# A graph network on one core: another place in ScalarE's queue for the copy of vector parts, and another wait for every second group of gathers

## What is computed

```
# first layer, per edge
x = silu(edge_radial @ W1 + b1)           # "layer 1": 8 -> 64
x = silu(x @ W2 + b2)                     # "layer 2": 64 -> 64
tpw = x @ W3 + b3                         # "layer 3": 64 -> 256 = W00, W110, W01, W10, each 8 x 8
hs_e, hv_e = h[src, :8], h[src, 8:]       # the gather: scalars, vectors of the source node
m0 = ALPHA * (einsum(hs_e * sh0, W00) + INV_SQRT3 * einsum(hv_e, sh1, W110))
m1 = ALPHA * (einsum(hs_e, sh1, W01) + einsum(hv_e * sh0, W10))
agg = segment_sum(concat(m0, m1), dst) / 4
x = layernorm(x + (h_self + agg))
# second layer
e = leaky_relu((x @ a1)[src] + (x @ a2)[dst])
x = layernorm(x + segment_softmax_sum(e, x[src], dst))
```

## Time and profile before

| | |
|---|---|
| median of 3 runs | 8619.93 us (8616.9 to 8624.02) |
| the profiled execution's own time | 8616.82 us |
| its span, first to last instruction | 8615.0 us |
| PE busy over the span | 6996.6 us (81%) |
| DVE busy | 6416.2 us (74%) |
| POOL busy | 5314.4 us (62%) |
| ACT busy | 2833.3 us (33%) |
| mean granted TensorE clock | 0.839 of full speed |

### The profile page before, as it was taken

How to read it: one execution, slowest core, us unless ns; L and a number is a source line. 1 busy time by engine, 2 the same in 40 slices (tenths; PEclk the granted TensorE clock), 3 DMA queues, 4 the chain that set the end, 5 groups by cost and what they waited for, 6 DMA issues and landing times.

```text
span 8615.0 us, 93580 instructions
## 1 busy us (share of the span) xinstructions
PE 6996.6 (81%) x26126; PEld 5354.8 (62%) x26126; DVE 6416.2 (74%) x11130; ACT 2833.3 (33%) x4982; POOL 5314.4 (62%) x5400
## 2 busy tenths in 40 slices
PE   6788888888787778888887715999999999999992
PEld 4555555555555555555555414888888888888881
DVE  7777777777777777777777734777777777777774
ACT  4444544454545445444444300111111111111110
POOL 5555555555556655555555466666666666666666
PEclk7777777777777777777777757999999999999996
DMA  2211212121212112111111211222222222222221
GB/s 61 40 39 39 41 39 40 39 41 38 40 38 41 38 39 41 39 39 31 34 33 33 48 24 35 48 52 48 49 50 47 52 47 52 48 52 47 52 48 27
DMA packets 318657, 363.23 MB, mean 42 GB/s; under 512 B 157446, under 2 KB 259510, under 8 KB 317962
## 3 DMA queue, kind: packets, MB, share of 16 engines
q0 software_dynamic: 175840, 136.07, 12.1%
q1 hardware_dynamic: 142794, 226.94, 8.4%
HBM read 251.38 MB, written 111.20 MB: 42 GB/s over the span
## 4 chain that ended last, share of the span: by engine, by line
PE 48%; issue 22%; DVE 14%; POOL 5%; DMA 5%; ACT 3%; another core or an unknown queue 2%; DVEq 0%; ACTq 0%; POOLq 0%; SPq 0%
PE tpw L661 26%; PE tpw L593 9%; DMA early<-in_x_wide,idx 5%; POOL early L476 4%; PE hid L661 4%; PE hid L583 4%; PE hid L579 3%; PE hid L602 2%; DVE prod L962 2%; DVE prod L953 2%; DVE hot L1253 1%; ACT hid L678 1%; ACT early L684 1%; POOL msgs L476 1%
## 5 line engine op out<-in xcount | busy, mean ns | idle before, releaser
L476 POOL DMA_INDIRECT early<-in_x_wide,idx x2870 | 2777.0, 968 | 2002.1 <-issue 1999.7
L476 POOL DMA_INDIRECT prod<-table,idx x2125 | 2144.8, 1009 | 1064.0 <-issue 592.8
L661 PE MATMUL tpw<-highs,hot 128*128 128x462 f32 x6125 | 2310.9, 377 | 91.7 <-DVE prod L1268 43.1
L661 PE MATMUL tpw<-lows,hot 128*128 128x462 f32 x6125 | 2291.1, 374 | 23.2 <-issue 22.1
L593 PE MATMUL tpw<-w3s,early 128*128 128x256 f32 x6252 | 2084.3, 501 | 3.1 <-DVE prod L962 3.1
L593 PEld LDWEIGHTS tpw<-w3s,early 128*128 128x128 f32 x6252 | 1545.1, 255 | 714.6 <-issue 357.9
L661 PEld LDWEIGHTS tpw<-highs,hot 128*128 128x128 f32 x6125 | 1165.3, 190 | 265.4 <-issue 60.7
L661 PEld LDWEIGHTS tpw<-lows,hot 128*128 128x128 f32 x6125 | 1158.9, 189 | 173.6 <-issue 45.7
L583 PE MATMUL hid<-hid,w2s 128*128 128x384 f32 x1042 | 559.7, 624 | 621.9 <-ACT hid L678 607.5
L684 ACT ACTIVATE early<-hid,b2s 64x384 f32<-64x384 f32 x1042 | 601.8, 578 | 1319.9 <-PE hid L583 1153.0
L579 PE MATMUL hid<-early,w1s 16*128 16x384 f32 x1044 | 663.0, 725 | 372.6 <-issue 193.1
(11 more groups left out here) (186 smaller groups left out, 8011.5 us busy)
## 6 DMA issues: line engine op xcount, KB each, us to landing
big<-qrows SPq DMA_DIRECT2D x126, 512.0 KB
scan<-prod SPq DMA_DIRECT2D x125, 425.0 KB
scan<-sums SPq DMA_DIRECT2D x130, 384.0 KB, 2.6
early<-in_x_wide,idx POOLq DMA_INDIRECT x2870
prod<-table,idx POOLq DMA_INDIRECT x2125
qbx<-qx SPq DMA_DIRECT2D x131, 128.0 KB
early<-in_radial_t SPq DMA_DIRECT2D x262, 48.0 KB
sh<-in_sh SPq DMA_DIRECT2D x131, 48.0 KB
```

The costliest lines, as they stand in the source:

```text
L476: return pool.indirect_dma_start(out=dest, out_offset=None, in_=source, in_offset=bass.IndirectOffsetOnAxis(ap=index, axis=0))
L661: mm = pe.matmul(found[i % BANKS][:, 0:BC], hot(c)[:, g, at:at + P], split(s, g), start=g == 0 and s == 0, stop=g == NBATCH - 1 and s == S ...
```

## The change

It has two parts. On ScalarE, `spread_hv` of a half no longer stands ahead of `first_hidden` at the end of the half before; it stands one step later, directly behind the `hidden` that belongs to layer 2 of the half's own odd group. On POOL, the gathers of an odd group g no longer wait until layer 3 of group g - 2 is done (`tpw_ready`); they wait until layer 1 of group g - 1 is done (`layers_done`). The wait for `tpw_used` is kept for all groups, and the even groups keep both waits.

```
             def gather_again(it, k, m, loads, all_tiles=False):
                 pool.wait_ge(tpw_used, it * SLOTS + k - 1)
-                pool.wait_ge(tpw_ready, it * SLOTS + k - 1)
+                if k % HALF == 0:
+                    pool.wait_ge(tpw_ready, it * SLOTS + k - 1)
+                else:
+                    pool.wait_ge(layers_done, it * SLOTS + k)
...
             def iteration(it, m, before, searching, loads=None):
...
                     hidden(g + 1, (k + 1) % 2)
+                    if k % HALF == 0:
+                        spread_hv(it, h, it > 1 if isinstance(it, int) else True)
                     if k == 0 and before is not None:
                         collect(it - 2, m, before, CT)
...
                         one_hot_x(it, m, loads, ((0, 1), (2, 3), (4, 5), (6,))[k])
-                    if k % HALF == HALF - 1:
-                        spread_hv(it + 1 if h else it, 1 - h, h == 0 and before is not None or h == 1 and not first and not last,
-                                  last and h == 1)
                     first_hidden(g + 2)
...
-            spread_hv(0, 0, False)
...
-            iteration(ITERS - 1, 1, ITERS // 2 - 2, False, None, True)
+            iteration(ITERS - 1, 1, ITERS // 2 - 2, False)
+            spread_hv(ITERS, 0, False, True)
```

More of the change, by code:

```diff
@@ L751, in collect, with iteration @@
                    .then_inc(sums_ready, 1)
-            def iteration(it, m, before, searching, loads=None, last=False):
+            def iteration(it, m, before, searching, loads=None):
                 first = before is None and m == 0
```

## The result

The changed kernel takes 8407.55 us (median of 4 runs, 8381.08 to 8418.97), the kernel before 8618.42 us beside it (8612.29 to 8624.02). The ratio is 0.9751, 95% interval [0.9726, 0.9777]. So it is faster, but by 211 us, not by the 992 that I forecast.

What follows compares the result with a forecast made beforehand. A chain through several engines, with layer 3 holding up the odd gathers, was taken to set 37.58 us an iteration. 99 periods at 29.9 and 28 at 29.3 save 760 + 232 = 992 us: 7628 us, range 7525 to 7900.

Steps and rivals of the forecast that it cites:

- POOL becomes the bound: Rival: if half of the 22 gathers took 1.53 us, an iteration would need 35.1 us, 8300 us in all; chance 0.05.
- Loops 1 and 3: Half B: DVE alone takes 14.66 us; PE and ACT, with `find_tile` waiting for `pick_x`, take 14.1 to 14.5.
- Step 2: PE and ACT in half A: layer 2 at 5.1 us after the spread, the next spread at 14.5; collect and one-hots 4.01.
- Steps 2 and 3: PE and ACT chains from spread to next spread: 14.5 us in half A, 14.1 to 14.5 in half B.
- 0.05 to PE: Half A: from `first_hidden` to the start of layer 2 on PE takes 0.05 us.
- I expect 2.4 GHz nearly always: PE's clock in the message stage: nearly always full, mean over 0.95, both layers 3 at 2.86 us.
- the clock keeps falling in each half: Rival: idle times of 1.35 and about 1 us keep one layer 3 per half at 1.2 GHz; 8134 us; chance 0.10.
- the forecast: Message stage: an iteration takes 29.9 us in 99 periods and 29.3 in the other 28, 29.77 on average.
- its loop: Half A over PE and ACT, from one spread to the next: 14.5 us at 2.4 GHz.

Runs made afterwards that it cites:

- e15: The changed kernel with one gather instead of five in each odd group, so messages are wrong: 8222.14 us, ratio 0.9487.
- e4: The changed kernel with the collect behind `first_hidden` at k = 0 instead of ahead of the one-hots: 8239.28 us, ratio 0.9563.
- e6: The changed kernel with the next layer 1 ahead of `find_tile` on TensorE instead of behind it: 8367.49 us, ratio 1.0024.
- e8: The changed kernel with the collect behind `first_hidden` and the next layer 1 ahead of `find_tile` on TensorE: 7714.01 us, ratio 0.9241.
- e5: The changed kernel with odd gathers stopped after their third tile until the layer 1 behind `find_tile` is done: 8014.86 us, ratio 0.9599.
- e1: The changed kernel with the old wait of the odd gathers for layer 3, so only the spread moves: 8315.0 us, ratio 0.9656.
- e12: The changed kernel with the collect behind `first_hidden`, the kernel of e4 measured again: 8237.02 us, ratio 0.9566.
- e11: The changed kernel with the collect behind `first_hidden` and odd gathers paused after their third tile until layer 1 is done: 8194.24 us, ratio 0.9514.

## Why the prediction was wrong

*The direction and the release of the gathers were right.* The odd gathers start 0.31 us after the even ones, and the spread doesn't wait for rows. The rival "POOL becomes the bound" is out: the mean gather takes 0.975 us over the kernel and POOL stands idle 1087 us in 3000. Single gathers do take 1.55 us beside L1007 (e15's row at 2008.98), an operation of VectorE with two inputs in SBUF. By the Trainium skill, "SBUF — State Buffer", section "SBUF: two separate sides", such an operation and a GpSimd one that reads SBUF block each other; the rows agree for the gathers that start beside one, and they are few: in the changed kernel 104 of 2478 took over 1.3 us (400 to 4300 us).

*The loops at the full clock were sized right where nothing else interferes.* Loops 1 and 3 gave 14.1 to 14.66 us for half B; e15 has 14.33.

*Step 2, "4.01 for the collect and one-hots", failed.* I took it from rows in which the collect did not wait, since `first_hidden` and `hidden` stood between it and the spread. Moved directly behind the spread it waits for the scan that VectorE runs after `bsum`, and `bsum` waits for that same spread. From the spread at 2025.77 to `first_hidden` at 2033.52 it is 7.75 us, less 0.46 for the spread 7.29: 3.3 more than the term; in the trace from 400 to 4300 us the 7.75 us are 7.7 to 7.9 in each of 109 halves A. The semaphore is in the code (`scanned`); I had listed what is queued behind the spread and not what each of it waits for. Taking this wait away gives back 1.33 us an iteration (e4); what it would give without the late signals is seen on the other kind of chip, from e6 to e8, 5.0 us, there with the fall of the clock behind it.

*Steps 2 and 3 also assume that a signal is there when the work is done ("0.05 to PE").* In the changed kernel the signal behind `find_tile` is a median 3.0 us late in 188 of 206 halves. That this hangs on the gathers is shown by e15. What it costs is shown for three kernels by the two kinds of chip, 2.0 to 4.0 us an iteration, as far as nothing else differs between them in this stage; the old kernel is worked out to have the same period on both: 8349.82 less 1.8 and 3427 is 4921 us to the last collect, 14 less than the 4934 of the old kernel's trace, and e5's first collect is 13 us earlier than the old kernel's. For the changed kernel itself it was not measured, since it never ran on the second kind. Why the old kernel has no late signal was not tested. The traces have this: its odd gathers start only behind layer 3, after a pause of 3 us, and `find_tile` ends during the second or third gather of a run in all 156 counted halves; in the changed kernel all 188 late signals have the eighth gather of a run or a later one there. It is no strict rule: 16 of the 18 signals on time have that too, and in e1 26 of the 122 late ones have the third or fourth.

*"I expect 2.4 GHz nearly always" failed, and mostly as a result of the two steps above.* The mean granted clock is 0.87. The idle time of 2.04 us ahead of layer 2 was to go; in its place stand 2.76 us behind the late signal (the row at 2023.63) and others like it. From 400 to 4300 us the odd layer 3 took 4.2 us or more in 131 of 217 halves. In 108 of them the idle time ahead of its layer 2 or layer 1 was over 1.6 us, and no odd layer 3 behind such an idle time took less. Of the other 109, with nothing over 1.6 us there, 23 took 4.2 us or more and 86 under 3.1, as here:

```profile
2008.66 0.90 PE L582 MATMUL hid<-early,w1s 16*128 16x384 f32 x2 [1.35 <-ACT early L687]
2009.49 2.86 PE L596 MATMUL tpw<-w3s,early 128*128 128x256 f32 x12
```

In e15, where no signal is late, all 229 took under 3.1 us. So laying the fall to the longer of the two idle times fits the changed kernel, and the rival "the clock keeps falling in each half" came true in 60% of the halves, but mostly not by its own cause. e8 shows that its cause can be enough, in another order.

So three things make up the 6.2 us by which the period lies above the forecast: the collect's wait, the late signals, and the low clock behind both. Their shares do not add up singly, since the waits hide each other: taking the collect's wait away gives 1.3 us beside late signals (e4) and 5.0 where there are none, in TensorE's other order (e6 to e8). e15, with no signal late, is 4.4 above the forecast, and half A alone is 5.3 above its loop: the collect's wait and the low clock behind it. The other 1.8 (35.96 - 34.15) I put down to the signals by difference only; e15 has fewer gathers too.

## What to carry to other kernels

When an instruction is moved in a queue, list for each one behind it the semaphore it waits for, and follow that back: here the chain led through VectorE to the moved instruction itself. A term read from a row holds only for the order in which it was read. A wait that is left out costs more than its length when the clock falls behind it: here 3.6 us of waiting came with 2.1 us of low clock (e15, half A). And if an experiment and its reference ran on different chips, run both again side by side before reading the edit's effect.

## What the runs showed of the hardware that I had not expected

- TensorE's signals reached the waiting engine up to 5.8 us after the matmuls' records ended (changed kernel; 8.5 in e4 and e12), and those behind came with it (2022.93, 2022.98, 2023.10), while GpSimd gathered in an unbroken run; with fewer gathers they were on time (e15: 228 of 228). In e11 226 of 227 signals came 1.6 to 2.3 us after the last gather. It happened on one kind of chip and in none of six traces of the other. The mechanism is open; so is whether it has to do with the semaphore events that the same traces lack, and whether the signals are late or the matmuls themselves, whose ends in the records are modelled.
- The stage behind the message stage takes 3427 us on one kind of chip and 3677 to 3732 on the other, with the same instructions.
- Gaps of 1.33 and 1.35 us on TensorE were followed by a layer 3 of 4.54 us, though PE had no longer gap in the iteration (e8; 165 of 235 odd layers 3). In e15 gaps of 1.26 to 1.35 us ahead of layer 1 were followed by the full clock in all 229.
